# Router logits as rows times four columns, a moved statistics step, biases split on VectorE, and new unit places in a selective scan

## Chip, cores and metric

One Trainium2 chip, one of its cores. The metric is the device time of one execution in microseconds; the median of three runs of the kernel before is 1462.75 us (1462.28 to 1463.16).

## What is computed

Two layers on x of shape (2, 2048, 256), float32. Layer 0: a layer norm `xn`; a gated linear recurrence (`h = f*h + z`, five 256x256 projections of an RMS-normed `xn`) whose output is added to `xn`; times the SiLU of a top-1 mixture of 4 experts. Layer 1: a layer norm; a selective scan (512 channels, 16 states); times the SiLU of a product with binarised weights. Cut to what matters here:

```python
# layer 0, router (x here is the layer norm of the input)
logits = x @ Wr + br                       # Wr is 256 x 4
probs = softmax(logits); top_w, top_idx = top_k(probs, 1)
out = expert[top_idx](x) * top_w           # silu(x@Wg) * (x@Wu) @ Wd
# layer 1, scan over time for each of 512 channels and 16 states n
dA = exp(d_t[..., None] * A)
state = dA * state + (d_t * u_t)[..., None] * b_t[:, None, :]
y_t = einsum('bdn,bn->bd', state, c_t)
y = ys + D * xc;  y = y * silu(z);  out = y @ W_out + b_out
```

## The kernel before, in words

Every engine has an instruction list of its own, in a fixed order; engines meet through semaphores. The work goes in chunks of 512 tokens (CHUNKS = 8), each of 4 tiles of 128 tokens.

Front end (0 to 49 us). VectorE makes the sums of each tile (`tile_sums`, L944), the `statistics` of two chunks at a time (L954 to L961), waits for GpSimd's power -0.5 (L586) and scales the rows (`scaled_tiles`, L967) into two staging tiles. TensorE turns them (`turn_inputs`, L1377), ScalarE copies them to `xT` (L692), TensorE makes the logits with the 4 columns of `w_r` as the loaded operand and 512 tokens moving (`logits`, L1386). ScalarE copies the 4x512 result (`copy_logits`, L697), and TensorE turns it back to token rows in `bank7` (`turn_logits`, L1394). TensorE's order: inputs of c, logits of c-1, turned logits of c-2. VectorE reads all logits at once (L1010), finds the maximum and the one-hot (L1019); TensorE then makes the ranks (L1412, L1413) between the third and the fourth projection of mixer chunk 0 (`project`, L1434). GpSimd also makes the power for all rows (L587), then splits the output weights and the biases into bfloat16 parts (`split_output` L564 to L568, `split_biases` L575 to L580). ScalarE scales the projection weights `w0` (L707) after chunk 4.

Mixer (49 to 205 us) and experts (205 to 588 us): 8 mixer chunks, then 35 slots of 128 rows through gate and up products (L1488) and down products (L1501).

Scan (600 to 1460 us). It goes in 8 turns q (one a chunk) of 64 units u; unit u = 4n + d is state n and channel block d. In each unit TensorE turns one block of `dbuT` into bank 4 or 5 (`spread`, L1671) one unit ahead, waiting for the scan before last; VectorE runs the scan (L1328); ScalarE makes `dA` (L864) and, four units ahead, a piece of `dbuT` (L853). GpSimd multiplies four finished scans by c (L674, `hc`), preceded by a small copy (L669). TensorE sums them into y (`add_up`, L1688). For the states n in `POOL_SPREADS` GpSimd makes `dbuT` (L656) four states ahead, in ScalarE's place. Between these, the constants at L49 to L88 say in which unit each engine does a step of the next chunk (or, in `Y` and `OUT`, of the one before): X, convolution and silu (`PE_X`, `ACT_X`, `DVE_CONV`, `ACT_SILU`), gate product (`PE_G`), low-rank steps (`PE_DT`, `PE_DL`, `PE_BC`, `PE_BT`), softplus and delta (`ACT_SOFT`, `DVE_DELTA`), du on GpSimd (`POOL_DU`, L640) and its turn (`PE_DUT` L1616, `ACT_DUT` L819), z products (`PE_Z`, L1562), output (`PE_YF`, `PE_OUT`), the residual on GpSimd (`POOL_RES`, L647). These steps share banks 6 and 7: a step waits until the one before it in its bank was read. `LAST_...` constants are for turn 7.

Of the kernel before, what the change touches and what calls it, by code (L numbers as in the profile page):

```python
# [83 lines left out]
POOL_DU = (8, 10, 11, 11)  # L84
POOL_RES = (12, 13)
SUM_AT = {(13, 0): 0, (13, 1): 2, (13, 2): 2, (13, 3): 4, (14, 0): 4, (14, 1): 4, (14, 2): 6, (14, 3): 6, (15, 0): 6,
          (15, 1): 7, (15, 2): 8, (15, 3): 8, (0, 0): 13, (0, 1): 14, (0, 2): 14, (0, 3): 14, (1, 0): 14, (1, 1): 15,
# [3 lines left out]
           "YF3": 1, "BC": 1, "OUT0": 1, "OUT1": 1, "Z0": 1, "Z1": 1, "Z2": 0, "Z3": 1}  # L91

# [24 lines left out]
LAST_TURNED = (6, 7, 4, 5)  # L117
IDLE_PRODUCTS = 12
# [25 lines left out]
def build(nc, a, out):  # L144
    with ExitStack() as ctx:
# [70 lines left out]
        logitsT = rt[0:NE].rearrange("p k t e -> p (k t e)").rearrange("p (u t) -> p u t", t=CH)  # L216
# [73 lines left out]
        logits_made = sem("logits_made")  # L290
        logits_copied = sem("logits_copied")
# [22 lines left out]
        eid_ready = sem("eid_ready")  # L314
        xg_loaded = [sem(f"xg_loaded{i}") for i in range(XG_BUFS)]
# [228 lines left out]
        def _(pool):  # L544
# [25 lines left out]
            def split_biases():  # L570
                pool.wait_ge(ld_small, 16 * 4)
                biases, taken = bias_f[:, 0:3 * D].rearrange("p (b d) -> p b d", d=D), bias_f[:, 3 * D:]
                for k in range(PARTS - 1):
                    part, less = (bias_b[0:PARTS, :, half, :] for half in range(2))
                    then(pool.tensor_copy(part, biases))  # L575
                    then(pool.tensor_tensor(less, part, taken[:, k:k + 1].unsqueeze(2).broadcast_to([PARTS, PARTS, D]),
                                            ALU.mult))
                    then(pool.tensor_tensor(biases, biases, less, ALU.add))
                for half in range(2):
                    pool.tensor_copy(bias_b[0:PARTS, :, half, :], biases).then_inc(split_ready, 1)  # L580

# [8 lines left out]
            split_biases()  # L590
# [96 lines left out]
        def _(act):  # L687
# [6 lines left out]
            def copy_logits(c, u):  # L694
                act.wait_ge(logits_made, c + 1)
                wait_past(act, logits_ready, c - 1)
                act.copy(logitsT[:, u, :], bank[4 + u][0:NE, :]).then_inc(logits_copied, 1)  # L697
# [11 lines left out]
            copy_logits(CHUNKS - 1, (CHUNKS - 1) % 2)  # L709
# [1144 lines left out]
```

## Time and profile before

| what | us |
|---|---|
| median of 3 runs | 1462.75 |
| the profiled execution | 1461.61 |
| its span | 1459.8 |
| TensorE busy (share of the span) | 1408.3 (96%) |
| VectorE busy | 1026.8 (70%) |
| GpSimd busy | 915.7 (63%) |
| ScalarE busy | 895.0 (61%) |
| chain that ended last: TensorE, VectorE, ScalarE | 75%, 11%, 8% |

PE is TensorE, PEld its weight loads, DVE VectorE, ACT ScalarE, POOL GpSimd. A name such as L1386 is a line of the kernel. In the timeline a line is start, duration, engine, line, operation, what it writes and reads, how often, and in brackets how long the engine had been idle and what ended that. Where several instructions stand in one line, the duration is from the first start to the last end. A float32 product appears as two load-and-product pairs.

### The profile page before, as it was taken

The numbers are of one execution on the slowest core, as the hardware profiler recorded it, in microseconds if no ns is written. First come the engines' busy times: TensorE is split into PE (matmuls) and PEld (weight loads), VectorE is DVE, ScalarE is ACT, GpSimd is POOL, SyncE is SP. The second block draws the span as 40 slices with busy tenths as digits, with TensorE's granted clock in tenths as the row PEclk, the third lists the DMA queues.
The fourth block names the chain that finished last, engine by engine and source line by source line (L and its number), as shares of the span: only waits on it lengthen the run. The fifth ranks groups of instructions, "written<-read, shape, count | busy, mean of one in ns | idle before, by whom it ended". The sixth has DMA issues, their size and how long they took to land.

```text
span 1459.8 us, 24233 instructions
## 1 busy us (share of the span) xinstructions
PE 1408.3 (96%) x9098; PEld 1128.4 (77%) x9128; DVE 1026.8 (70%) x1373; ACT 895.0 (61%) x1465; POOL 915.7 (63%) x463
## 2 busy tenths in 40 slices
PE   6999999999999999989899999999999999999998
PEld 3454469999999999457677877878778778788887
DVE  7655542233332322588898998998998998998997
ACT  4211121111111111389989989999899899899993
POOL 4422211222222222149989989989989989899895
PEclk9999999999999999999999999999999999999999
DMA  9921136666766764110121121211211211201211
GB/s 310 395 79 47 58 115 241 254 262 232 258 259 244 271 243 155 41 59 29 45 73 45 45 74 43 73 59 43 82 37 45 88 44 45 73 31 44 88 55 47
DMA packets 53299, 172.70 MB, mean 118 GB/s; under 512 B 6079, under 2 KB 32319, under 8 KB 48326
## 3 DMA queue, kind: packets, MB, share of 16 engines
q1 hardware_dynamic: 46054, 150.22, 29.1%
q0 software_dynamic: 7136, 21.01, 4.3%
q8 instruction: 71, 1.16, 0.3%
q14 instruction: 38, 0.31, 0.1%
HBM read 141.78 MB, written 31.00 MB: 118 GB/s over the span
## 4 chain that ended last, share of the span: by engine, by line
PE 75%; DVE 11%; ACT 8%; issue 4%; POOL 1%; DMA 0%; SPq 0%; DVEq 0%; ACTq 0%; POOLq 0%
PE bank L1488 17%; PE bank L1671 10%; PE bank L1688 9%; PE bank L1434 9%; PE bank L1501 8%; DVE hst L1328 5%; PE bank L1562 4%; PE bank L1592 3%; ACT dA L864 2%; PE bank L1628 2%; PE bank L1600 2%; PE bank L1463 2%; PE bank L1555 2%; PE bank L1573 1%; ACT dbuT L853 1%
## 5 line engine op out<-in xcount | busy, mean ns | idle before, releaser
L1328 DVE TENSOR_TENSOR_SCAN hst<-dA,carry,bank 128x512 f32<-128x512 f32 x512 | 633.2, 1270 | 54.1 <-PE bank L1671 48.7
L674 POOL TENSOR_TENSOR hst<-hst,c_bc 128x2048 f32<-128x2048 f32 x127 | 579.0, 4563 | 23.0 <-DVE hst L1328 8.3
L864 ACT ACTIVATE dA<-delta,negA 128x512 f32<-128x512 f32 x512 | 360.0, 718 | 2.2 <-DVE hst L1328 1.4
L1671 PEld LDWEIGHTS bank<-ident,dbuT 128*128 128x128 f32 x2048 | 243.3, 141 | 135.8 <-issue 74.1
L1671 PE MATMUL bank<-ident,dbuT 128*128 128x128 f32 x2048 | 312.8, 276 | 15.7 <-DVE hst L1328 10.5
L1688 PE MATMUL bank<-ident,hst 128*128 128x128 f32 x2016 | 291.0, 273 | 0.0
L853 ACT ACTIVATE dbuT<-duT,bT 128x512 f32<-128x512 f32 x386 | 276.4, 717 | 1.5 <-PE bank L1671 1.4
L1488 PEld LDWEIGHTS bank<-f_sb,w_gu 128*128 128x128 f32 x2240 | 255.5, 192 | 2.7 <-ACT f_sb L736 1.0
L1488 PE MATMUL bank<-f_sb,w_gu 128*128 128x128 f32 x2240 | 256.0, 275 | 0.7 <-ACT f_sb L736 0.7
L1688 PEld LDWEIGHTS bank<-ident,hst 128*128 128x128 f32 x2016 | 234.1, 141 | 0.0
L615 POOL TENSOR_TENSOR x_sb<-x_sb,neg_half 128x1 f32<-128x1 f32 x35 | 23.0, 657 | 260.2 <-DVE x_sb L1151 260.2
L740 ACT ACTIVATE sg_z<-bank 128x512 f32<-128x512 f32 x70 | 41.9, 598 | 215.9 <-PE bank L1488 215.9
L1434 PE MATMUL bank<-xT,w 128*128 (+1 forms) x320 | 139.2, 593 | 0.0
L1434 PEld LDWEIGHTS bank<-xT,w 128*128 128x128 f32 x320 | 60.0, 190 | 71.9 <-issue 71.7
L656 POOL TENSOR_TENSOR dbuT<-duT,bT 128x2048 f32<-128x2048 f32 x31 | 112.2, 3619 | 2.2 <-PE bank L1671 2.2
L596 POOL DMA_INDIRECT sorted_x<-xn_st,idx x32 | 35.8, 1119 | 110.5 <-DVE idx L1074 103.2
L1143 DVE TENSOR_TENSOR x_sb<-x_sb 128x256 f32<-128x256 f32 x35 | 14.9, 425 | 98.7 <-ACT x_sb L751 98.7
L1132 DVE TENSOR_TENSOR xT<-sg_z,bank 128x512 f32<-128x512 f32 x36 | 24.8, 688 | 83.3 <-ACT sg_z L740 60.3
L751 ACT ACTIVATE x_sb<-bank,x_sb 128x256 f32<-128x256 f32 x35 | 16.6, 475 | 99.7 <-PE bank L1501 99.7
L1132 DVE TENSOR_TENSOR sg_a<-sg_z,bank 128x512 f32<-128x512 f32 x34 | 23.4, 688 | 76.0 <-ACT sg_z L740 50.1
L1555 PE MATMUL bank<-xn2T,w_in 128*128 128x512 f32 x128 | 66.6, 612 | 1.2 <-DVE xn2T L1224 1.2
L1501 PE MATMUL bank<-w_d,xT 128*128 x288 | 65.2, 380 | 0.8 <-ACT x_sb L751 0.8
(210 smaller groups left out, 1715.7 us busy)
## 6 DMA issues: line engine op xcount, KB each, us to landing
w_gu<-in_w_gu SPq DMA_DIRECT2D x35, 2048.0 KB
c_bc<-c_rows SPq DMA_DIRECT2D x64, 512.0 KB, 3.7
sorted_x<-sg_a SPq DMA_DIRECT2D x12, 387.0 KB, 11.3
x_sb<-sorted_x SPq DMA_DIRECT2D x35, 129.0 KB
x_sb<-in_x SPq DMA_DIRECT2D x8, 512.0 KB, 7.3
w_d<-in_w_d SPq DMA_DIRECT2D x1, 4096.0 KB, 21.1
x_mix<-x_sb SPq DMA_DIRECT2D x1, 4096.0 KB, 32.1
x_mix<-rt SPq DMA_DIRECT2D x8, 512.0 KB
```

The lines of the kernel that those rows point to most:

```text
L656: pool.tensor_tensor(dbuT[at % DBU_BUFS][:], duT[q % B][:], bT[q % B][:, :, n:n + 1].broadcast_to([P, TPC, DI]), ALU.mult).then_inc(dbuT_p ...
L674: pool.tensor_tensor(h[:], h[:], c, ALU.mult).then_inc(hc_ready, 1)
L853: act.activation(dbuT[(DS * q + n) % DBU_BUFS][:, i, :], duT[q % B][:, i, :], ACT.Copy, scale=bT[q % B][:, i, n:n + 1]).then_inc(dbuT_act, 1)
L864: act.activation(dA[:, at % DA_BUFS, :], delta[q % B][:, d, :], ACT.Exp, scale=negA[:, d, n:n + 1]).then_inc(dA_ready, 1)
L1328: v.tensor_tensor_scan(h[:, d, :], dA[:, at % DA_BUFS, :], bank[4 + u % 2][:], carry1[q % B][:, n, d:d + 1], ALU.mult, ALU.add).then_inc(s ...
L1434: ins = pe.matmul(bank[2 + w][:], w0[:, w, k, s * P:(s + 1) * P], xT[:, bass.ds((c * KB + k) * CH, CH)], start=(k == 0), stop=(k == KB - 1))
L1488: ins = pe.matmul(bank[1 + 2 * half + n][:, i * P:(i + 1) * P], w_gu[j % 2][:, n, k, at:at + P], xgT[:, k, :], start=(k == 0), stop=(k == ...
L1501: ins = pe.matmul(bank[7][:, 0:D], hidT[j % 2][:, i, :], w_d[:, bass.ds(e * (FB * D) + i * D, D)], start=(i == 0), stop=(i == FB - 1))
L1555: ins = pe.matmul(M[:], w_in[:, k, d * P:(d + 1) * P], xn2T[(t + 1) % B][:, k, :], start=(k == 0), stop=(k == KB - 1))
L1562: ins = pe.matmul(M[:], xn2T[(t + 1) % B][:, k, i * P:(i + 1) * P], w_in[:, k, DI:2 * DI], start=(k == 0), stop=(k == KB - 1))
L1671: ins = pe.transpose(bank[4 + u % 2][:, i * P:(i + 1) * P], dbuT[(DS * q + n) % DBU_BUFS][:, i, d * P:(d + 1) * P], ident[:])
L1688: ins = pe.matmul(bank[i][:, d * P:(d + 1) * P], hst[n % STATE_BUFS][:, d, i * P:(i + 1) * P], ident[:], is_transpose=True, start=False, s ...
```

## The change

The router logits are made with the turned rows as the loaded operand (128x128) and the four columns of `w_r` moving, straight into their place in `bank7`; the copy and the turning back go. TensorE's order of inputs and logits is new, ten products on the raw rows are put first, and `w0` is scaled after chunk 5. VectorE makes the last statistics between the scaling of chunks 4 and 5. The biases are split on VectorE, with one operation in place of two. In the scan stage the units of many steps change, and GpSimd makes the states 4, 7, 10, 11 in every turn. The line with `CHUNKS // 2` is the condition under which ScalarE scales `w0`. Cut to its core:

```diff
-POOL_SPREADS = (6, 7, 10, 11)
-LAST_SPREADS = (6, 7, 11)
+POOL_SPREADS = (4, 7, 10, 11)
+LAST_SPREADS = (4, 7, 10, 11)
-PE_X = (0, 1, 2, 4, 7, 8, 9, 10)
+PE_X = (0, 1, 2, 3, 7, 8, 9, 10)
-PE_DT = (22, 23, 25, 27)
-PE_DL = (28, 34, 37, 41)
-PE_BC = (27, 28, 30, 31)
-PE_BT = 44
-PE_DUT = (51, 52, 54, 56)
-PE_Z = (50, 51, 54, 55, 57, 58, 60, 61)
+PE_DT = (21, 23, 24, 26)
+PE_DL = (28, 33, 37, 41)
+PE_BC = (29, 30, 31, 32)
+PE_BT = 47
+PE_DUT = (49, 50, 53, 54)
+PE_Z = (50, 52, 53, 56, 57, 58, 60, 61)
-PE_YF = (20, 32, 36, 37)
-PE_OUT = (38, 40, 43, 44, 46, 47, 48, 49)
+PE_YF = (20, 32, 35, 37)
+PE_OUT = (39, 40, 43, 44, 46, 47, 48, 49)
-ACT_X = (5, 6, 11, 13)
-ACT_SILU = 25
-ACT_SOFT = (33, 38, 42, 45)
-ACT_DUT = (55, 56, 58, 59)
-ACT_YF = (26, 35, 39, 41)
-DVE_CONV = (3, 4, 5, 6, 7, 8, 10, 11, 12, 13, 14, 15)
+ACT_X = (5, 6, 12, 18)
+ACT_SILU = 24
+ACT_SOFT = (33, 38, 43, 44)
+ACT_DUT = (52, 53, 56, 57)
+ACT_YF = (30, 35, 40, 41)
+DVE_CONV = (3, 4, 5, 6, 7, 8, 9, 11, 12, 13, 14, 15)
-DVE_DT = 28
-DVE_DELTA = (31, 36, 40, 44)
-DVE_BC = 35
-DVE_BT = 47
+DVE_DT = 27
+DVE_DELTA = (31, 36, 41, 44)
+DVE_BC = 33
+DVE_BT = 48
-POOL_DU = (8, 10, 11, 11)
-POOL_RES = (12, 13)
+POOL_DU = (7, 9, 10, 11)
+POOL_RES = (9, 11)
...
+WARM = 10
...
-                if c == CHUNKS // 2:
+                if c == CHUNKS // 2 + 1:
...
-            two_scaled(2)
+            one_scaled(2, 0)
             statistics(3)
+            one_scaled(2, 1)
             two_scaled(3)
+            for k in range(PARTS - 1):
+                part = bias_b[0:PARTS, :, 0, :]
+                then(v.tensor_copy(part, biases))
+                then(v.scalar_tensor_tensor(biases, part, taken[:, k:k + 1], biases, ALU.mult, ALU.add))
+            for half in range(2):
+                v.tensor_copy(bias_b[0:PARTS, :, half, :], biases).then_inc(bias_ready, 1)
...
+            pe.wait_ge(ld_x[0], 16)
+            for i in range(WARM):
+                pe.wait_ge(tile_stats, min(i + 1, 2 * TPC))
+                pe.matmul(bank[7][:, 0:D], x_sb[:, 0, 0:P], x_sb[:, 0, :], start=True, stop=True)
...
-                    ins = pe.matmul(bank[4 + u][0:NE, :], w_r[:, k, :], xT[:, at:at + CH], start=(k == 0),
-                                    stop=(k == KB - 1))
+                    for k in range(KB):
+                        rows = (c * KB + k) * CH + i * P
+                        ins = pe.matmul(bank[7][:, at:at + NE], xT[:, rows:rows + P], w_r[:, k, :], start=(k == 0),
+                                        stop=(k == KB - 1))
...
+            for c in (0, 2):
+                turn_inputs(c, 0)
+                turn_inputs(c + 1, 1)
+                logits(c)
+                logits(c + 1)
+            turn_inputs(4, 0)
+            logits(4)
+            turn_inputs(5, 1)
+            for c in (5, 6):
+                turn_inputs(c + 1, (c + 1) % 2)
+                logits(c)
+            logits(7)
```

Turn 7 keeps the old `PE_YF`, `PE_OUT`, `ACT_YF` and results. The units of the sums of n = 13 to 15 and 0 move by at most one (`SUM_AT`). TensorE waits for `bias_ready` beside `split_ready` before the first mixed output.

## Rows read from the trace of the kernel before

**Rows 1.** Windows: stretch, its us, each engine's busy us, PEclk, DMA, GB/s
```profile
205.00:588.00 383.00, 381.51 (x2892) 366.17 (x2891) 118.71 (x283) 67.62 (x140) 93.18 (x102) 1.00 0.64 236
634.00:747.00 113.00, 103.74 (x667) 78.32 (x667) 102.58 (x99) 103.53 (x168) 99.02 (x42) 0.97 0.14 48
...
953.00:1056.00 103.00, 101.35 (x691) 82.42 (x692) 95.81 (x96) 96.05 (x155) 96.65 (x43) 1.00 0.18 57
```

**Rows 2.** Timeline 19 to 35 us: start, us, engine, line, out<-in, [idle before <-releaser]
```profile
19.39 1.09 PE L1377 MATMUL bank<-ident,xn_st 128*128 128x128 f32 x8
20.41 1.88 PE L1386 MATMUL bank<-xT,w_r 128*4 128x512 f32 x4
22.22 0.32 PEld L1394 LDWEIGHTS bank<-ident,rt 4*128 4x128 f32 x4 [0.86 <-issue]
29.38 2.61 ACT L707 ACTIVATE w<-w,cols 128x1280 f32<-128x1280 f32 x2
30.25 5.43 POOL L587 TENSOR_TENSOR rstd<-tmp,neg_half 128x32 f32<-128x32 f32 x1
30.32 1.39 DVE L967 TENSOR_SCALAR xn_st<-x_sb,mean,rr 128x256 f32<-128x256 f32 x4 [1.75 <-POOL rr L586]
32.91 0.19 DVE L993 TENSOR_TENSOR tmp<-tmp,rr 128x32 f32<-128x32 f32 x1
```

**Rows 3.** Timeline 40 to 63 us, all engines
```profile
40.79 1.98 PE L1434 MATMUL bank<-xT,w 128*128 128x512 f32 x4
43.25 0.29 DVE L1010 TENSOR_TENSOR rt<-bank,tmp 128x128 f32<-128x128 f32 x1 [6.97 <-PE bank L1394]
45.34 1.44 DVE L1017 TENSOR_TENSOR rt<-rt,small 128x128 f32<-128x128 f32 x1
48.54 0.49 PE L1412 MATMUL bank<-rt,z_sb 128*128 128x128 f32 x2 [1.79 <-DVE rt L1019]
49.08 13.90 PE L1434 MATMUL bank<-xT,w 128*128 128x512 f32 x32
```

**Rows 4.** Chain of work from 226.47 us: start, us, what, how many
```profile
226.47 7.14 PE bank L1488 x64
```

**Rows 5.** Waits, turn 3 (953.2 to 1056.7 us): total us, times, longest
```profile
PEld bank L1671 <- DVE hst L1328: 4.4, 13, 0.6
```

**Rows 6.** Turn 3, VectorE, ScalarE and TensorE in the timeline
```profile
951.92 0.59 ACT L781 COPY xpad<-bank 128x512 f32<-128x512 f32 x1 [2.52 <-PE bank L1555]
959.07 1.27 DVE L1328 TENSOR_TENSOR_SCAN hst<-dA,carry,bank 128x512 f32<-128x512 f32 x1
959.32 0.57 ACT L781 COPY xpad<-bank 128x512 f32<-128x512 f32 x1
971.17 1.28 DVE L1328 TENSOR_TENSOR_SCAN hst<-dA,carry,bank 128x512 f32<-128x512 f32 x1
...
1036.01 0.60 PE L1616 MATMUL bank<-ident,xpad 128*128 128x128 f32 x4
```

**Rows 7.** Turn 3, GpSimd in the timeline
```profile
964.61 0.19 POOL L669 COPY carry<-hst 128x4 f32<-128x4 f32 x1 [3.56 <-DVE hst L1328]
...
973.27 0.19 POOL L669 COPY carry<-hst 128x4 f32<-128x4 f32 x1
...
1029.99 2.53 POOL L640 TENSOR_TENSOR xpad<-delta,xc 128x512 f32<-128x512 f32 x2
```

**Rows 8.** Turn 0, TensorE in the timeline
```profile
721.40 0.66 PE L1616 MATMUL bank<-ident,xpad 128*128 128x128 f32 x4 [1.32 <-POOL xpad L640]
```

**Rows 9.** Turn 7, VectorE's and GpSimd's timelines
```profile
1374.22 4.82 DVE L1328 TENSOR_TENSOR_SCAN hst<-dA,carry,bank 128x512 f32<-128x512 f32 x4
1381.90 4.55 POOL L674 TENSOR_TENSOR hst<-hst,c_bc 128x2048 f32<-128x2048 f32 x1
...
1411.63 31.62 POOL L674 TENSOR_TENSOR hst<-hst,c_bc 128x2048 f32<-128x2048 f32 x7
```

**Rows 10.** Chain of work from 1443.49 us
```profile
1443.49 0.47 PE bank L1750 x4
```

More of the change, by code:

```diff
@@ L91 @@
            "YF3": 1, "BC": 1, "OUT0": 1, "OUT1": 1, "Z0": 1, "Z1": 1, "Z2": 0, "Z3": 1}
+LAST_SPREADS = (4, 7, 10, 11)
+LAST_PE_YF = (20, 32, 36, 37)
+LAST_PE_OUT = (38, 40, 43, 44, 46, 47, 48, 49)
+LAST_ACT_YF = (26, 35, 39, 41)
+LAST_RESULT = (45, 50)
+LAST_SUMS = {0: (14, 15, 16, 16), 1: (17, 18, 19, 19), 12: (57, 58, 59, 60), 13: (61, 62, 63, 63)}
 SUMS_AT = [[] for _ in range(UNITS)]
@@ L314, in build @@
         eid_ready = sem("eid_ready")
+        bias_ready = sem("bias_ready")
         xg_loaded = [sem(f"xg_loaded{i}") for i in range(XG_BUFS)]
@@ L568, in split_output @@
                 pool.tensor_copy(wo_b[:, 2], wo_r).then_inc(split_ready, 1)
[L570 to L580, printed above, removed]
             quarter = TILES // 4
@@ L692, in turn_inputs @@
                     act.copy(xT[:, at:at + CH], bank[2 * u + k][:]).then_inc(xrT_ready, 1)
[L694 to L697, printed above, removed]
             turn_inputs(0, 0)
@@ L838, in slot @@
                     act.preload_act_table_set("natural_log_exp_and_others")
-                if q >= 1 and u in ACT_YF:
-                    turn_y(q, ACT_YF.index(u))
+                turns = ACT_YF if q + 1 < CHUNKS else LAST_ACT_YF
+                if q >= 1 and u in turns:
+                    turn_y(q, turns.index(u))
             def spread_du(q, p):
@@ L972, in two_sums, with one_scaled @@
                 tile_sums(2 * i + 1)
+            def one_scaled(i, u):
+                v.wait_ge(rr_ready, i + 1)
+                scaled_tiles(2 * i + u, u)
             def two_scaled(i):
-                v.wait_ge(rr_ready, i + 1)
-                scaled_tiles(2 * i, 0)
-                scaled_tiles(2 * i + 1, 1)
+                one_scaled(i, 0)
+                one_scaled(i, 1)
             two_sums(0)
@@ L1271, in slot @@
                         gate_y(q - 1, DVE_GATE.index(u))
-                    if u in DVE_RESULT:
-                        result(q, DVE_RESULT.index(u))
+                    results = DVE_RESULT if q + 1 < CHUNKS else LAST_RESULT
+                    if u in results:
+                        result(q, results.index(u))
                 if q + 2 < CHUNKS and u in DVE_XN:
@@ L1379, in turn_inputs, with logits @@
                     ins.then_inc(xr_turned, 1)
-            def logits(c, u):
+            def logits(c):
                 pe.wait_ge(xrT_ready, KB * c + KB)
-                wait_past(pe, logits_copied, c - 1)
-                for k in range(KB):
-                    at = (c * KB + k) * CH
-                    ins = pe.matmul(bank[4 + u][0:NE, :], w_r[:, k, :], xT[:, at:at + CH], start=(k == 0),
-                                    stop=(k == KB - 1))
-                ins.then_inc(logits_made, 1)
-            def turn_logits(c, u):
-                pe.wait_ge(logits_copied, c + 1)
                 for i in range(TPC):
                     at = (c * TPC + i) * NE
-                    ins = pe.transpose(bank[7][:, at:at + NE], logitsT[:, u, i * P:(i + 1) * P], ident[0:NE, 0:NE])
+                    for k in range(KB):
+                        rows = (c * KB + k) * CH + i * P
+                        ins = pe.matmul(bank[7][:, at:at + NE], xT[:, rows:rows + P], w_r[:, k, :], start=(k == 0),
+                                        stop=(k == KB - 1))
                 ins.then_inc(logits_ready, 1)
-            turn_inputs(0, 0)
-            turn_inputs(1, 1)
-            logits(0, 0)
-            for c in range(2, CHUNKS):
-                turn_inputs(c, c % 2)
-                logits(c - 1, (c - 1) % 2)
-                turn_logits(c - 2, c % 2)
-            logits(CHUNKS - 1, (CHUNKS - 1) % 2)
-            turn_logits(CHUNKS - 2, CHUNKS % 2)
+            for c in (0, 2):
[10 more added lines that the diff above has]
+            logits(7)
             def ranks():
@@ L1450, in mixer @@
                 if isinstance(c, int) and c == 0:
-                    pe.wait_ge(split_ready, 3)
+                    pe.wait_ge(split_ready, 1)
+                    pe.wait_ge(bias_ready, 2)
                 pe.wait_ge(gated_ready, SB * c + SB)
@@ L1642, in slot @@
                     dt(q, PE_DL.index(u))
-                if q >= 1 and u in PE_YF:
-                    turn_y(q, PE_YF.index(u))
+                turns = PE_YF if q + 1 < CHUNKS else LAST_PE_YF
+                if q >= 1 and u in turns:
+                    turn_y(q, turns.index(u))
                 if q + 1 < CHUNKS and u in PE_BC:
                     low_rank(q, "BC", XR - P, P, PE_BC.index(u))
-                if q >= 1 and u in PE_OUT:
-                    out_proj(q, *divmod(PE_OUT.index(u), TPC))
+                outs = PE_OUT if q + 1 < CHUNKS else LAST_PE_OUT
+                if q >= 1 and u in outs:
+                    out_proj(q, *divmod(outs.index(u), TPC))
                 if q + 1 < CHUNKS and u == PE_BT:
```

15 lines of the change are left out of this document (5 added, 10 removed).

## The prediction

> **What bounds the kernel now.** I read the stretches first, then the front end's timeline, then one whole turn of the scan. In the expert stage TensorE is busy 381.51 of 383 us, and the mixer before it runs its products without a gap [rows 1, 3]: whatever arrives earlier at 49 us reaches the scan stage whole. In the front end (to 49 us) two things end last in turn. TensorE works off a backlog: each chunk costs it 1.02 us of turned inputs (19.39 to 20.41), 1.81 of logits (to 22.22) and 0.34 of turning them back (to 22.56), 3.17 in all [rows 2], and it gets to its first projection at 40.79; VectorE has waited 6.97 us for the logits by 43.25, and TensorE then waits 1.79 for the one-hot before its rank product at 48.54 [rows 3]. In the scan stage a turn takes 103.5 us, of which TensorE is busy 101.35 in a window of 103 [rows 1]. Its load unit waits only 4.4 us a turn for VectorE's scans [rows 5], mostly in the first units, where VectorE's convolutions make it the slower engine. New places can win part of these waits and no more.
>
> **Front end.** VectorE. The last statistics are made after the first of two chunks' scaling. The 1.75 us wait for GpSimd's power [rows 2] then has 1.3 us (four scaled tiles; 1.39 with its tail) of scaling over it, so the last scaling ends at about 31.65, not 33.0.
>
> TensorE. Turning back (0.34) goes. The logits become 4 tiles x 2 halves; the trace shows two load-and-product pairs for each float32 product, so 16 pairs a chunk. The cost of a pair with four columns isn't in the trace. From above: 128x128 loads under 128 columns of products come every 7.14/64 = 0.11 us [rows 4]. From below: four loads of 128 columns before 4-column products take 0.32, 0.08 each [rows 2]. I take 0.10, between two near ends: 1.6 us a chunk (1.3 to 1.8). With 1.0 for the turned inputs that is 2.6 against 3.17, and TensorE no longer has a backlog: it follows VectorE.
>
> The Trainium skill (TensorE: Matmul & The Clock Gate, LDWEIGHTS) has a load cost columns/1.2 ns whatever the rows: 107 ns here, 1.7 us a chunk; the 0.08 of a load of four rows [rows 2] speaks against it. By the page the first projection would start 0.2 us later than below.
>
> Tail. Chunk 5 is turned by about 30.5 and copied by 31.1 (its logits' neighbour, chunk 4, goes first). ScalarE now scales the projection weights there, 2.61 us [rows 2], to 33.7. Then it makes four copies of 0.53 (to 35.75). Logits 6 run 34.75 to 36.35, logits 7 to 37.95 (37.0 with 0.08). The first projection starts there instead of at 40.79. Three projections follow: 32 records in 13.9, so 1.74 each [rows 3], to 43.15; ranks 0.54 (48.54 to 49.08), to 43.7. Before: 49.08. That is 5.4 us, if VectorE's one-hot is there by 43.15.
>
> VectorE to the one-hot. The bias split comes to it: two casts and two three-operand operations on 768 elements, then two casts. No row shows them on VectorE. From above, 256 elements take 0.34 (1.39 for four) [rows 2], so 768 take 1.0: six, 6.3 with their waits. From below 0.19 each, the row of 32 elements: 1.2. I take 4.5, because the 256-element row is the nearer and casts can be quicker. From 31.65 it ends at 36.2 (32.9 to 38.0); the scale product of the logits takes 0.7 more, with the second power ready at about 34.5. The logits arrive at 38.0, so it is hidden but for the upper end. From the logits to the one-hot it took 5.3 (43.25 to 48.54), with one operation of 1.44 where its like takes 0.29 [rows 3]: GpSimd's bias operations ran beside it, and they go. I take 3.1, so 41.2: 2 us of slack (none at 5.3 and the upper end; then 0.9 of the 5.4 is lost). Next late is TensorE itself. GpSimd's split of the output weights still ends (38.9) before ScalarE's first sigmoid. The ten new products on the raw rows end by about 13.4 even at half speed and touch nothing that ends last: 0, at worst 0.5 hidden under the sums. No DMA moves, save that the expert loads are issued 5 us earlier. Front: -5.4, from -6.3 to -4.5.
>
> What VectorE meets from GpSimd: a two-operand operation took 0.19 at 32.91, inside GpSimd's power of 5.43 (30.25 to 35.68) [rows 2]. So the power doesn't block it. The Trainium skill (SBUF — State Buffer, SBUF: two separate sides) says that VectorE operations with two SBUF inputs and GpSimd operations lock each other out for a whole instruction; by it the split would wait for the power's end (about 34.4) and end near 39, and the front would win some 4.5 to 5.4. That row speaks against it for the power, the 1.44 for it elsewhere.
>
> **Scan places, turns 1 to 6.** (a) ScalarE's third copy goes from unit 11 to 12, 0.61 later, and VectorE's convolution of it from unit 10 to 9. In the old timing the tap would be ready at 959.32+0.61+1.34 = 961.3 and VectorE there at 959.07+1.19 = 960.26: 1.0 short, in the part where VectorE is the slower. But ScalarE had idled 2.52 for TensorE's second product [rows 6], which moves up a unit, 1.4 us. So the tap is at 959.9: hidden, 0.35 in hand. (b) GpSimd makes the spread of n=4 in the 3.56 us gap before n=2, instead of n=6 after it; n=3 then waits for the scan of unit 15 (971.17+1.19) and starts at 972.5 instead of 973.27 [rows 6, 7]: 0.77. From there to the last two du products it took 56.72. (c) Ahead of the last du now stand one du and one residual more, 1.25 each (2.53 for two): 972.5+56.72+3x1.25 = 1033.0. TensorE turns it two units earlier: 1036.01 [rows 6] less two spreads with sums (1.74), less a half z product (0.87), less 0.3 that smoother units win = 1033.1. The slack falls from 3.5 to 0.1 us. What TensorE gains ahead of that point is capped there: -0.3 a turn, -1.8 in six. Bounds: all 1.7 us of TensorE's waits gone, or 0.5 later. (d) The other shifts by a unit or two keep TensorE's sum of work over a turn; that their producers come in time too is what the bounds are for.
>
> Turn 0: TensorE waited until 721.40 for the third du in unit 54 [rows 8]. The fourth now comes at about 721.3 in the same unit, but half a z product and a turn (1.3) that followed are already done: -1.3 (0 to -1.6).
>
> Turn 7: GpSimd works without a gap to 1443.25, and TensorE takes its last product at 1443.49 [rows 9, 10]. It gets four spreads for three: +3.6. The one made early fills a gap, so n=3 starts with the scan's end at 1379.05 instead of 1381.90: -2.85. Net 0.75 less the 0.2 of slack: +0.55 (0 to +1.1).
>
> **The sum:** -5.4 -1.3 -1.8 +0.55 = -8.0 us. The profiled execution took 1461.61 with a span of 1459.8; the span becomes 1451.8, the execution 1453.6. The median of the runs is 1.14 above the profiled one: 1454.8.
>
> **Rivals.**
> - A late fourth du: GpSimd's row of three is 0.5 us longer and every turn waits for it, so a turn changes by +0.2 instead of -0.3, turn 0 too: -5.4+0.55+7x0.2 = -3.5, 1459.3. For: slack 0.1. Against: all its terms are rows. 0.17, on both sides of the bound.
> - The late tap of (a): ScalarE doesn't come earlier. 7x1.08 = +7.6; -5.4+0.55+7.6 = +2.8: 1465.5. Against: its idle of 2.52. 0.08.
> - The turned logits don't do what they say: the load isn't hidden and costs its whole recorded time, up to 0.19: 3.0 us a chunk, TensorE keeps a backlog of 4.0 a chunk from 22.6 to 46.1, +2.7 at 49 us; with the scans 1463. Against: the 0.11 of rows 4. 0.07.
> - The scan gains all it can: 1.7x7 = -12: 1445. Against: the du chain. 0.06.
 Against: between them lie 2.6 us of work a chunk. 0.06.
>
> **How the numbers follow.** Forecast 0.56. About 0.2% (2.9 us) is what a measurement can tell. Faster: the forecast, the full gain and half of the du case, 0.71. Same: the other half, the unhidden loads, part of the tap case, 0.20. Slower: the clock and the rest, 0.09. Range 1449.0 to 1463.5: the forecast with its bounds (front 0.9 each way, turns -1.7 to +0.5), the du and the load cases; outside stay the full gain, the tap and the clock.
>
> **What would show it.** The rank product at 43 to 44 us without a wait for VectorE; logits of 1.3 to 1.8 us a chunk; VectorE's bias operations under 6.3 together and before the logits; the expert stage 5.4 earlier with its length unchanged; turns of 103.2 us, TensorE's turn of the fourth du with a wait of a few tenths for GpSimd; GpSimd's last product ending 0.8 later against turn 7's start. I am wrong if the one-hot is late, the turns grow, or PEclk falls before 49 us.

## The result

| | before | after |
|---|---|---|
| median of 9 runs each, us | 1462.71 (1461.04 to 1463.16) | 1465.83 (1464.21 to 1470.40) |
| ratio, 95% interval | | 1.0029 (1.0021 to 1.0038) |
| profiled execution / its span, us | 1461.61 / 1459.8 | 1464.96 / 1462.9 |
| mean granted TensorE clock | 0.997 | 0.987 |

By the medians the change makes the kernel 3.1 us slower (the interval of the ratio is 3.1 to 5.6 us); the forecast was 1454.8 (1449.0 to 1463.5), 11 us lower than what was measured.

**Where the time went.** I follow five marks through the traces: the projections that start behind the rank product, the first expert's product, the same convolution step of VectorE in each turn (its distance is the length of a turn), and the start of VectorE's last operation. In us:

| kernel | projections | to first expert | to turn 0 | turn 0 | turns 1 to 5, each | turns 6 and 7 | end |
|---|---|---|---|---|---|---|---|
| before | 49.08 | 158.04 | 436.64 | 101.48 | 103.55 | 194.29 | 1457.26 |
| after | 53.01 | 158.04 | 436.59 | 101.65 | 103.20 | 195.04 | 1460.33 |

So the front end lost 3.93, turn 0 0.17 and the last two turns 0.75; turns 1 to 5 won 0.35 each. The front end alone turns the forecast round: -5.4 was expected.

The same stretches of the front end in the windows of the kernel after (columns as in [rows 1]; before had a granted clock of 1.00 in all of them):

```profile
16.00:19.00 3.00, 2.84 (x26) 2.75 (x25) 3.00 (x10) 0.04 (x1) 1.34 (x1) 1.00 0.99 373
19.00:23.00 4.00, 3.44 (x19) 3.44 (x19) 3.79 (x17) 1.75 (x3) 0.74 (x1) 0.57 1.13 294
23.00:27.00 4.00, 4.00 (x33) 4.00 (x34) 3.84 (x15) 0.59 (x2) 0.90 (x1) 0.87 1.14 287
27.00:31.00 4.00, 3.33 (x17) 2.92 (x15) 3.08 (x11) 1.17 (x2) 3.46 (x2) 0.50 1.08 275
31.00:36.00 5.00, 5.00 (x25) 5.00 (x26) 1.27 (x4) 1.94 (x3) 3.66 (x1) 0.50 1.21 228
41.00:50.00 9.00, 9.00 (x26) 6.00 (x27) 5.22 (x15) 1.60 (x3) 0.82 (x1) 0.51 0.95 399
```

PEclk (third from the end) falls to 0.5, the 1.2 GHz level, in most of 19 to 50 us (36 to 41, not shown, has 0.84), although TensorE is busy for nearly all of it. TensorE's and VectorE's timelines of the kernel after, to be held against [rows 2, 3]:

```profile
15.21 3.63 PE L1391 MATMUL bank<-w_r,xT 128*128 128x4 f32 x32
19.56 1.97 PE L1381 MATMUL bank<-ident,xn_st 128*128 128x128 f32 x8 [0.72 <-DVE xn_st L952]
22.82 3.93 PE L1391 MATMUL bank<-w_r,xT 128*128 128x4 f32 x32
38.78 6.19 PE L1391 MATMUL bank<-w_r,xT 128*128 128x4 f32 x32
44.83 7.90 PE L1435 MATMUL bank<-xT,w 128*128 128x512 f32 x12
53.01 7.46 PE L1435 MATMUL bank<-xT,w 128*128 128x512 f32 x17
...
36.02 0.93 DVE L986 CAST bias_b<-bias_f 3x768 bf16<-3x768 f32 x1
36.99 1.84 DVE L987 SCALAR_TENSOR_TENSOR bias_f<-bias_b,bias_f 3x768 f32<-3x768 bf16 x1
45.11 0.29 DVE L1009 TENSOR_TENSOR rt<-bank,tmp 128x128 f32<-128x128 f32 x1 [1.61 <-PE bank L1391]
```

At the full clock 32 pairs with four columns take 3.63, or 0.113 each; the last 32 take 6.19. The turned inputs double from 1.09 to 1.97, and the 12 records of the first projections take 7.90 where 5.2 was expected. The one-hot is quick (2.4 from 45.11; 5.3 before) and TensorE does not wait for it, as forecast, but all of it stands 7 us later than forecast (45.11 for 38.0).

### The profile page after: what moved, and what is told of

Read it like the earlier page. It is cut to its first block, busy times and chain, and to the rows that moved or that the text cites. A ratio compares the mean times of both kernels' runs of the same rounds, so it can differ in the third digit from the quotient of the medians.

```text
span 1462.9 us, 24412 instructions
## 1 busy us (share of the span) xinstructions
PE 1419.6 (97%) x9212; PEld 1152.5 (79%) x9212; DVE 1030.1 (70%) x1379; ACT 886.7 (61%) x1453; POOL 911.0 (62%) x456
## 4 chain that ended last, share of the span: by engine, by line
PE 79%; DVE 8%; ACT 5%; issue 4%; POOL 2%; DMA 0%; POOLq 0%; SPq 0%; DVEq 0%; ACTq 0%
PE bank L1489 17%; PE bank L1674 11%; PE bank L1691 11%; PE bank L1435 10%; PE bank L1502 8%; DVE hst L1328 4%; PE bank L1593 4%; PE bank L1563 3%; PE bank L1629 3%; ACT dA L849 2%; PE bank L1601 2%; PE bank L1574 2%; POOL hst L665 1%; PE bank L1465 1%; ACT dbuT L838 1%
## 5 line engine op out<-in xcount | busy, mean ns | idle before, releaser
L1674 PEld LDWEIGHTS bank<-ident,dbuT 128*128 128x128 f32 x2048 | 246.3, 142 | 141.4 <-issue 89.3
L838 ACT ACTIVATE dbuT<-duT,bT 128x512 f32<-128x512 f32 x382 | 271.7, 712 | 11.7 <-PE bank L1674 11.6
L647 POOL TENSOR_TENSOR dbuT<-duT,bT 128x2048 f32<-128x2048 f32 x32 | 115.7, 3614 | 0.8 <-PE bank L1674 0.7
L735 ACT ACTIVATE x_sb<-bank,x_sb 128x256 f32<-128x256 f32 x35 | 16.6, 473 | 99.7 <-PE bank L1502 99.7
```

The source lines that it names most:

```text
L647: pool.tensor_tensor(dbuT[at % DBU_BUFS][:], duT[q % B][:], bT[q % B][:, :, n:n + 1].broadcast_to([P, TPC, DI]), ALU.mult).then_inc(dbuT_p ...
L838: act.activation(dbuT[(DS * q + n) % DBU_BUFS][:, i, :], duT[q % B][:, i, :], ACT.Copy, scale=bT[q % B][:, i, n:n + 1]).then_inc(dbuT_act, 1)
L1674: ins = pe.transpose(bank[4 + u % 2][:, i * P:(i + 1) * P], dbuT[(DS * q + n) % DBU_BUFS][:, i, d * P:(d + 1) * P], ident[:])
```

## The experiments

All times beside runs of the kernel before on the same chip (medians 1462.06 to 1462.53).

| kernel | median (range), us | ratio, 95% interval |
|---|---|---|
| new scan places only | 1461.11 (1459.01 to 1461.51) | 0.9988 (0.9979 to 0.9998) |
| new front end only | 1468.68 (1465.36 to 1471.61) | 1.0048 (1.0033 to 1.0064) |
| after, 128 columns moved | 1457.75 (1454.97 to 1458.37) | 0.9966 (0.9954 to 0.9977) |
| after, old logits | 1460.05 (1459.84 to 1460.94) | 0.9988 (0.9979 to 0.9998) |
| after, old logits, no early products | 1459.72 (1459.13 to 1460.20) | 0.9984 (0.9975 to 0.9994) |
| after, no early products | 1471.09 (1465.36 to 1473.96) | 1.0060 (1.0040 to 1.0081) |
| 128 columns, three last spreads | 1457.34 (1455.62 to 1457.91) | 0.9962 (0.9948 to 0.9977) |
| 128 columns, late expert loads | 1455.70 (1455.39 to 1456.57) | 0.9956 (0.9942 to 0.9970) |
| 128 columns, biases on GpSimd | 1459.38 (1458.08 to 1460.85) | 0.9979 (0.9969 to 0.9988) |
| 128 columns, no early products | 1456.58 (1455.84 to 1458.27) | 0.9961 (0.9947 to 0.9975) |
| combination | 1455.40 (1454.50 to 1456.70) | 0.9955 (0.9941 to 0.9969) |
| combination, old places | 1457.07 (1456.44 to 1457.80) | 0.9965 (0.9953 to 0.9977) |
| combination, residuals at 12 and 13 | 1453.94 (1453.38 to 1454.23) | 0.9943 (0.9928 to 0.9958) |
| before, late expert loads | 1461.97 (1461.27 to 1462.54) | 1.0001 (0.9991 to 1.0010) |

**1. How many columns the products move.** The kernel after, with each logits product 128 columns wide; 124 of them multiply zeros, and what they give is overwritten by later tiles or read by nobody.

```
+ v.memset(w_rw[:], 0.0)                       # VectorE, at the start
+ v.tensor_copy(w_rw[:, :, 0:NE], w_r[:])      # behind the second two_sums
- pe.matmul(bank[7][:, at:at + NE], xT[:, rows:rows + P], w_r[:, k, :], ...)
+ pe.matmul(bank[7][:, at:at + P], xT[:, rows:rows + P], w_rw[:, k, :], ...)
```

> The kernel after, but each logits product moves 128 columns and not 4: VectorE zeroes a 128x2x128 tile and copies the router's 4 columns into it, TensorE writes 128 columns of PSUM of which the first 4 count. Same waits, same order, same number of products; the 120 idle columns fit beside the weight load (an estimate from 0.136 us for a turned 128x128 against 0.113 for a pair with 4 columns). Theory 1 (the clock fell because the products moved only four columns): the granted clock stays at 1.00 in 16 to 50 us, the first projection stands near 36 to 38.5 us, the total is 1457 to 1459 us. Rival 2 (it fell because TensorE waits for VectorE between the chunks): the clock falls as in the kernel after, the first projection stands at 44 to 46 us, 1465.5 to 1467 us. Rival 3 (the biases on VectorE are what is late, not the clock): the clock stays full but the first projection moves by no more than the 2 us of the turned inputs, 1463 to 1464 us.

Windows and timeline of this kernel:

```profile
16.00:19.00 3.00, 2.62 (x24) 2.43 (x22) 3.00 (x10) 0.00 (x0) 1.02 (x1) 1.00 0.98 370
19.00:23.00 4.00, 3.56 (x30) 3.32 (x31) 3.79 (x17) 2.15 (x4) 1.06 (x1) 1.00 1.12 268
31.00:36.00 5.00, 4.45 (x40) 4.21 (x39) 4.89 (x8) 4.69 (x7) 4.92 (x3) 1.00 1.17 205
...
14.89 3.74 PE L1400 MATMUL bank<-w_rw,xT 128*128 128x128 f32 x32
19.25 1.09 PE L1388 MATMUL bank<-ident,xn_st 128*128 128x128 f32 x8 [0.62 <-DVE xn_st L955]
38.44 5.32 PE L1444 MATMUL bank<-xT,w 128*128 128x512 f32 x12
44.04 13.90 PE L1444 MATMUL bank<-xT,w 128*128 128x512 f32 x32
```

TensorE is about as busy as in the kernel after (2.62 and 3.56 against 2.84 and 3.44) and has about the same wait before the second chunk pair's turned inputs (0.62 against 0.72), but the clock stays at 1.00. The extra columns cost 0.11 per 32 pairs. The first projection starts at 38.44, the next ones at 44.04: 5.04 us before the kernel before, 8.97 before the kernel after (0.32 of this stands at the first turned inputs already, 12.76 against 13.08: executions start a little differently). This is theory 1, and the median is 8 us under that of the kernel after. The forecast's front end, 37.95 and 43.7, was right but for its clock.

**2. Waits, the early products, and why the times lie so far apart.** The old form of the logits in the frame of the kernel after, with and without the ten early products, and the kernel after without them.

```
- turn_inputs(c, 0); ...; logits(c); logits(c + 1)              # after
+ turn_inputs(c, c % 2); logits(c - 1, ...); turn_logits(c - 2, ...)   # as before
```
```
- for i in range(WARM): ... pe.matmul(bank[7][:, 0:D], x_sb[:, 0, 0:P], x_sb[:, 0, :], ...)
```

> The kernel after with the old form of the logits (w_r as the weights, 512 columns moved, ScalarE's copy, four turns per chunk) and its old order on TensorE and ScalarE; the early products on TensorE, the statistics between two chunks' scaling, the biases on VectorE and the new scan places stay. Theory 1: the granted clock is full throughout the front end as in the kernel before, so the first projection stands where before had it or up to 2 us later (the bias split of VectorE is then what ends last), 38 to 43 us from the span's start; 1460 to 1464 us. Rival 2 (the moved statistics or the early products make the clock fall): it falls here too and the time is 1465 us or more.

> The kernel after with the old form of the logits and without its ten early products. Theory (in the run with them the fall at 19 to 23 us was that of a TensorE that had waited 2.38 us for VectorE, because its turned inputs had ended sooner): the first turned inputs take 1.9 us per 8, TensorE is not idle in 16 to 19 us, the clock is 1.00 in 19 to 23 us, and the next projections start within 0.5 us of 48.29; 1460 us. Rival (the fall there has nothing to do with the wait): it is there in this run too.

> The kernel after without its ten early products. Theory 1 (the four-column products alone let the clock fall): the granted clock still falls to half in 26 to 50 us, the next projections start at 52 to 53.5 us, 1465 to 1466 us. Rival (the fall needs the early products' head start and TensorE's waits that follow from it): the clock stays full, the next projections start near 44, 1457.5 us.

> The four-column form without the early products, one more profiled execution. Theory (a longer execution is one in which the clock stays at half for longer, or falls again behind the front end): a time of 1469 us or more comes with longer stretches at half clock than in the first profile. Rival (the further 5 us are lost elsewhere, with the clock full): they are in the mixer, where the first chunk's scatter ends later, or in the scan's turns. If the execution is a short one (1465 to 1466 us) nothing is learnt.

> The new front end with the old scan places, one more profiled execution. The same two theories: at 1469 us or more, either longer stretches at half clock in the front end, or a loss behind it with the clock full; at 1465 to 1467 us nothing is learnt.

With the old form and the early products, TensorE idles 2.38 us and the clock then is at half once, which theory 1 had not expected:

```profile
16.00:19.00 3.00, 0.88 (x3) 0.00 (x0) 3.00 (x10) 0.57 (x1) 1.05 (x1) 1.00 1.00 371
...
19.00:23.00 4.00, 3.73 (x11) 1.88 (x12) 3.79 (x17) 1.17 (x2) 1.04 (x1) 0.57 1.12 275
...
19.27 1.97 PE L1391 MATMUL bank<-ident,xn_st 128*128 128x128 f32 x8 [2.38 <-DVE xn_st L962]
```

Without the early products that wait is 0.87 and the clock 1.00 from its first entry at 16.6 us to the end of the front end; the next projections start at 46.84 instead of 48.29. That was over 0.5 earlier, because at the full clock TensorE works its backlog off sooner. So with the old form the fall goes with the wait, and the wait comes with the early products. In the kernel after neither is the cause. Without the early products its clock falls in the same stretches (0.57 in 19 to 23, 0.50 in 27 to 36), the next projections start at 53.16, and TensorE has no gap ahead of the first fall:

```profile
16.00:19.00 3.00, 3.00 (x30) 3.00 (x28) 3.00 (x10) 0.72 (x2) 0.97 (x1) 1.00 1.00 370
19.00:23.00 4.00, 4.00 (x24) 4.00 (x24) 3.79 (x17) 1.61 (x3) 1.11 (x1) 0.57 1.11 262
```

The times of a four-column kernel lie 6 to 9 us apart from execution to execution, those of the others 1 to 3.5. Without early products two of five executions took 1465.4 and 1465.6 and three 1471.1 to 1474.0, so the median misses my 1465 to 1466. A second profiled execution without early products took 1472.02 us (the one of the kernel with the new front end took 1466.96, a short one, and showed nothing new). Its windows and timeline:

```profile
19.00:23.00 4.00, 4.00 (x20) 4.00 (x21) 3.79 (x18) 0.00 (x0) 0.26 (x1) 1.00 1.10 321
23.00:27.00 4.00, 4.00 (x20) 4.00 (x21) 3.52 (x11) 1.65 (x3) 1.38 (x1) 1.00 1.10 293
...
17.00 6.83 PE L1387 MATMUL bank<-w_r,xT 128*128 128x4 f32 x32
23.68 1.95 PE L1377 MATMUL bank<-ident,xn_st 128*128 128x128 f32 x8
52.64 7.28 PE L1431 MATMUL bank<-xT,w 128*128 128x512 f32 x12
60.20 13.90 PE L1431 MATMUL bank<-xT,w 128*128 128x512 f32 x32
```

The first 32 pairs take 6.83 instead of 3.84: TensorE keeps from its start to about 42 us the pace of the 1.2 GHz level. PEclk prints 1.00 there only because the trace's list of granted clocks has no entry yet: its first one, with the full level, is at 42.8 us, and at 15.9 in the first execution; the pace changes at these times. So in the long execution the clock rose 27 us later. The next projections start at 60.20 instead of 53.16. Of these 7.0 us, 0.85 stand at the first turned inputs already (13.56 against 12.71), and the rest is the clock; from there to the end both take 1407.2 to 1407.4. The theory (longer at half) holds. Of the kernel after and of the one with the new front end only short executions were profiled. Their long ones have the lower mean clocks (0.984 at 1470.4 against 0.988 at 1464.2; 0.985 at 1471.6 against 0.988 at 1466.1), which fits more time at half, but where it lies is not shown.

**3. The two halves apart.**

```
places only:    before + the new constants and the LAST_ ones
front end only: after  - the new constants
```

> The kernel before with the new places of the scan stage alone (the front end is the old one: old logits, statistics and biases). Theory A (the front end lost 3.9 us and the scan places gave back some 0.8 net, each by itself): the first scan starts where it did before (633.7), turns 0 to 6 end about 1.5 to 2.5 us early, the last turn gives about 0.9 back; 1461 to 1462 us, some 1.3 us under before. My forecast's own sum for these parts: turn 0 -1.3, turns 1 to 6 -1.8, turn 7 +0.55, so 1460.2. Rival (the extra half-clock stretch in turn 0 of the kernel after is a consequence of the new places): turn 0 gains nothing here either and 1461.5 or more comes out; if it is a consequence of the late front end, turn 0 gains its 1.3 here.

> The kernel after with the old places of the scan stage: only the front end is new. Theory A: the first projection stands at 44.8 us from the span's start against 40.8 before, the granted clock is at half in about 19.5 to 23 and 26 to 50 us, and everything behind runs 3.9 us late: 1466.6 us. Rival (the scan places and the front end are not independent): under 1465 or over 1468.5.

| kernel | projections | to first expert | turn 0 | turns 1 to 5, each | turns 6 and 7 |
|---|---|---|---|---|---|
| places only | 49.11 | 158.04 | 101.78 | 103.25 | 195.00 |
| front end only | 52.91 | 158.04 | 102.08 | 103.54 | 194.27 |

Turns of 103.2 belong to the places, the late projections to the front end. The front end alone came out at 1468.68, above its expected 1466.6 and the bound of the rival; its profiled execution is a short one with 1466.10, and three of its six took 1470.8 to 1471.6 (experiment 2). Turn 0 gains nothing with the new places alone, with the clock at 0.57 in 715 to 719 where it had been 1.00: the half-clock stretch in turn 0 comes with the new places, as the rival had it. Turn 0 is also where the halves don't add up: +0.30 and +0.60 against +0.17; the part on the prediction says why.

**4. Who takes back what the front end won.** In experiment 1 the way from the projections to the first expert takes 159.81, not 158.04. VectorE's timeline names the wait:

```profile
74.15 1.38 DVE L1076 TENSOR_SCALAR xn_st<-x_sb,mean,rstd 128x256 f32<-128x256 f32 x4 [5.03 <-DMA sorted_x<-xn_st,idx]
```

The second chunk's rows need the buffer that the first chunk's scatter (GpSimd's DMA that puts the rows in the order of the experts) reads. The kernel before has the same wait, shorter:

```profile
76.24 1.38 DVE L1070 TENSOR_SCALAR xn_st<-x_sb,mean,rstd 128x256 f32<-128x256 f32 x4 [2.08 <-DMA sorted_x<-xn_st,idx]
```

The scatter shares the 16 DMA engines with two loads of 2 MB; the DMA share is 1.10, 1.04 and 0.97 in the five-us stretches from 60 to 75. Two kernels with these loads behind the second mixed chunk:

```
- load_up(0); load_up(1)
- with sp.Fori(0, CHUNKS - 1) as c: store_mixed(c)
+ store_mixed(0); store_mixed(1); load_up(0); load_up(1)
+ with sp.Fori(2, CHUNKS - 1) as c: store_mixed(c)
```

> The 128-column form of the logits, and the two loads of expert weights (2 MB each, issued at 53.5 us) issued behind the second mixed chunk's store (about 82 us), so that the first chunk's four scatters have the DMA engines nearly for themselves. Theory A (the mixer took back 1.8 of the 5.0 us won in front because VectorE waited until 74.15 us for the first chunk's scatter, and that landing is set by what the 16 DMA engines move until then): VectorE's wait of 5.0 us before the second chunk's rows falls to under 2 us, the first expert's product stands 1.5 to 2 us earlier (202.0 against 203.85), 1456.0 us. Rival (the scatter takes its time whatever else moves): the wait stays at 4 to 5 us and the time at 1457.7 us. Second rival (the expert weights are then late at the first expert): no, they have 110 us of cover; if it were so the first expert would start later than 203.85.

> The kernel before, with the two loads of expert weights alone issued behind the second mixed chunk's store. Theory A (in the kernel before the first chunk's scatter is waited for too, 2.08 us, but the projections of TensorE cover all of it but 0.25): the wait is gone and the first expert's product stands at 206.9 to 207.1 against 207.12, the time is the same, 1462.2 to 1462.5 us. Rival (the scatter costs the kernel before as much as it costs the one with the fast front end): 1460.7 us.

VectorE and the windows with the 128-column form and late loads:

```profile
69.38 1.38 DVE L1078 TENSOR_SCALAR xn_st<-x_sb,mean,rstd 128x256 f32<-128x256 f32 x4
...
65.00:70.00 5.00, 5.00 (x13) 2.28 (x12) 4.29 (x8) 0.64 (x2) 0.33 (x1) 1.00 0.44 164
```

The wait is gone, the share falls to 0.44, and the way to the first expert is 158.04 again (44.38 to 202.42): 1.77 us, and 2.05 in the medians. In the kernel before the same edit takes away its wait of 2.08 as well and gives nothing (158.03; ratio 1.0001): there TensorE's projections cover it. Theory A holds in both.

**5. Biases on GpSimd or on VectorE.**

```
- VectorE:  tensor_copy, scalar_tensor_tensor (twice), two tensor_copy
+ GpSimd:   split_biases() behind split_output(), as before
```

> The 128-column form of the logits, with the biases split on GpSimd as in the kernel before. Theory A (with the clock full, VectorE's split of 6.7 us ends within 1 us of the last logits, so it costs at most that; and the mixer's wait for the scatter eats what is won in front): the next projections start at 43.2 to 43.6 us against 44.04, the first expert's product stands where it was (203.85), total within 0.4 us of 1457.7. Rival (the split on VectorE is worth what the change put it there for): the front end is not earlier or the ranks wait for GpSimd, 1458.5 us or more.

I expected almost nothing and it costs 1.6 us in the medians. In the marks it is 2.8 (projections 45.09, first expert at 206.69 for 203.85), of which 0.6 stand at the first turned inputs already (13.36 for 12.76), so 2.2. VectorE and GpSimd in its timeline:

```profile
40.58 1.19 DVE L1022 TENSOR_TENSOR rt<-rt,rs 128x128 f32<-128x128 f32 x1
42.01 1.61 DVE L1025 TENSOR_TENSOR rt<-rt,small 128x128 f32<-128x128 f32 x1
45.85 3.47 DVE L1036 TENSOR_TENSOR_SCAN rt<-rs,rt 128x32 f32<-128x32 f32 x4
...
40.16 1.46 POOL L582 TENSOR_TENSOR bias_b<-bias_b,bias_f 3x768 bf16<-3x768 bf16 x1
41.70 1.76 POOL L584 TENSOR_TENSOR bias_f<-bias_f,bias_b 3x768 f32<-3x768 f32 x1
44.42 1.46 POOL L582 TENSOR_TENSOR bias_b<-bias_b,bias_f 3x768 bf16<-3x768 bf16 x1
```

A VectorE operation of 0.29 ends 0.15 us behind GpSimd's two-operand operation that was under way: 41.77 behind 41.62, and 43.62 behind 43.46. The four scans take 3.47 instead of 1.01. The Trainium skill (SBUF — State Buffer, SBUF: two separate sides) says that a VectorE operation with two SBUF inputs waits for the whole of such a GpSimd operation; for these operations the trace agrees ([rows 2] has one of 0.19 inside GpSimd's power, which did not wait). So this part of the change is worth 1.6 to 2.2 us once the front end is early: the rival was right against me. The forecast had this gain in its one-hot (5.3 to 3.1); it was my expectation for this run that forgot it.

**6. The last turns, the residuals, the places.** The combination is the 128-column form with late loads, three spreads on GpSimd in the last turn and no early products.

```
a. 128 columns:  LAST_SPREADS = (4, 7, 10, 11) -> (6, 7, 11)
b. 128 columns:  without the ten early products
c. combination
d. combination:  all old scan places
e. combination:  POOL_RES = (9, 11) -> (12, 13)
```

> The 128-column form of the logits, and in the last turn the three spreads on GpSimd of the kernel before (6, 7, 11) and not four. Theory A (what the last turn loses is its fourth spread on GpSimd): everything up to the last turn as in the run of the 128-column form (its last turn's start is where it was), turns 6 and 7 cost 0.7 less, 1457.0 us. Rival (turn 6's lateness, not the last turn's own places, is what costs): the same 1457.7 us.

> The 128-column form of the logits without the ten early products on x. Theory A (the early products do nothing for the clock, which stood at full in the kernel before without them): clock 1.00 from 11 to 50 us, first projection at 38.4, 1457.7 us. Rival (they lift the clock before the first turned inputs): the first turned inputs and products run at half clock, the front end is 1 to 3 us later unless VectorE hides it, 1458 to 1460 us.

> The 128-column logits, the loads of expert weights behind the second mixed chunk, three spreads on GpSimd in the last turn, and no early products. Theory A (each saving stands by itself: front end 5.0, mixer 1:1 again, turns 1 to 5 0.3 each, last turn 0): 1455.0 us, 7.5 under before. Rival (what is won in front changes where the clock falls in turn 0, which has been worth up to 0.8 either way): 1454.5 to 1456.

> The kernel of the run before this one, with all the old places of the scan stage. Theory A (the new places are worth 0.33 a turn in turns 1 to 5, about nothing in turn 0): a turn of 103.55 us and not 103.2, 1.7 us more than that run, 1456.7 us. Rival (my forecast's turn 0 gain of 1.3 is there with a fast front end): 3 us more.

> The same combination, with the two residuals of GpSimd at 12 and 13 as in the kernel before and not at 9 and 11. My forecast's theory (the residual at 11 stands ahead of the fourth du and makes TensorE's turn of it wait some 0.2 us a turn): turns 1 to 6 are 0.2 us shorter each, 1.0 to 1.2 us in all. Rival (the 0.2 us wait of TensorE is not on the path of the scan): the same within 0.3 us. Second rival (the places 12 and 13 then collide with the next turn's spreads): slower by up to 1 us a turn.

| kernel | projections | to first expert | turn 0 | turns 1 to 5, each | turns 6 and 7 | end |
|---|---|---|---|---|---|---|
| 128 columns | 44.04 | 159.81 | 102.22 | 103.20 | 195.04 | 1453.70 |
| a | 44.57 | 159.81 | 101.99 | 103.25 | 194.25 | 1453.52 |
| b | 44.20 | 159.23 | 101.20 | 103.23 | 195.04 | 1452.39 |
| c | 44.16 | 158.04 | 102.01 | 103.20 | 194.19 | 1451.00 |
| d | 44.48 | 158.03 | 101.44 | 103.53 | 194.34 | 1452.56 |
| e | 44.50 | 158.04 | 101.21 | 103.00 | 194.25 | 1449.60 |

(a) The fourth spread on GpSimd costs the last two turns 0.79, about the 0.75 that the forecast set against it; the medians (1457.34 and 1457.75) are too near to tell. (b) The early products do lift the clock before the first turned inputs (1.07 instead of 1.94), which I had not expected, but VectorE hides it: the projections start at 44.04 with them and at 44.20 without. (d) Old places: 0.33 a turn more in turns 1 to 5, as forecast, and no gain of 1.3 for the new ones in turn 0. (e) The units 12 and 13 take away TensorE's wait for the fourth du. TensorE's load unit, waits in turn 3, the kernel after and then c (e has no such row):

```profile
PEld bank L1617 <- POOL xpad L631: 0.2, 1, 0.2
...
PEld bank L1624 <- POOL xpad L636: 0.2, 1, 0.2
```

A turn goes from 103.20 to 103.00 in all five, the 0.2 of that row. The ends of c and e are 1.4 apart: 1.0 from these turns, 0.8 from turn 0, where the clock was at half for less time, and 0.4 lost at the start and the end. With e the kernel takes 1453.94, 8.2 us under the kernel before: faster than both.

## Why the prediction was wrong, point by point

**TensorE's clock: the step that failed.** The sum ran all of the front end at the full clock. The half-clock rival stood at 0.06 with 1475; it is what happened, at a lower price: 8.97 us (53.01 against 44.04), where the rival had 20 over the forecast. Its reason was wrong as well. I named TensorE's waits; experiment 1 keeps the waits and about the busy time and the clock stays, and without the early products it falls with no gap ahead of it (experiment 2), so it is the four moved columns. The text's own argument against the rival, "between them lie 2.6 us of work a chunk", does not hold for four-column products: the clock fell with 4.00 of 4.00 us busy (experiment 2). No row of before shows 128x128 loads with four moved columns; 0.06 was far too low for an operation form that I had only priced by its duration.

**The front end otherwise.** Pair 0.10 expected, 0.113 measured. Tail: 37.95 and 43.7 expected, 38.44 and 44.04 measured with the clock full, a gain of 5.04 for 5.4 (the 37.0 given for pairs of 0.08 adds up to 37.3). One-hot 3.1 expected, 2.4 measured. The bias split was sized at 4.5, with 6.3 as its upper end; it takes 7.1 (36.02 to 43.11), and 6.75 in experiment 1. The narrow three-operand operations take 1.01 alone and 1.84 or 2.00 beside GpSimd's split of the output weights: the contention that I had put aside by a row of GpSimd's power. It was hidden all the same, as the sum had it.

**"Whatever arrives earlier at 49 us reaches the scan stage whole": wrong by 1.77.** The mixer passes on a delay whole (3.93 in the kernel after), but not this gain: behind busy DMA engines the scatter comes only 2.09 earlier (74.15 against 76.24) where VectorE comes 5 earlier. The wait of 2.08 stood in the trace of before, and I had not priced what lies under its cover. With the clock full, the change comes to 1457.75, not 1454.8.

**Turn 0: the wait went, the time didn't.** TensorE's wait of 1.32 for GpSimd [rows 8] is gone. In its place the second du's turn waits for ScalarE's copy, longer than before. TensorE in the kernel before and then after:

```profile
717.70 0.63 PE L1616 MATMUL bank<-ident,xpad 128*128 128x128 f32 x4 [0.79 <-ACT duT L819]
...
718.30 0.63 PE L1617 MATMUL bank<-ident,xpad 128*128 128x128 f32 x4 [2.10 <-ACT duT L803]
718.77 1.79 PE L1563 MATMUL bank<-w_in,xn2T 128*128 128x512 f32 x2
```

0.79 for the second du and 1.32 for the third make 2.11 before, 2.10 in one piece after. Measured from the start of the turn, TensorE comes to the second du 4.6 earlier (716.20 less 647.64 against 716.91 less 643.76), but ScalarE's copy of the first, whose bank it needs, only 3.3 earlier. And right behind this wait the granted clock is at half from 718.9 to 722.3: the z product takes 1.79 where it takes 1.02 at 723.06. That costs about 1.7, an estimate from the starts of this product and the three operations behind it against the same ones in the next unit. All 13 executions with the new places have the one wait of 2.10 to 2.14 and the fall behind it, all 5 with the old ones two shorter waits and no fall. So the step -1.3 failed twice: I asked when the fourth du would be made and not when the bank of the second would be free, and I ran the turn at the full clock. Over all kernels turn 0 took 101.4 to 102.1 with old places and 101.0 to 102.2 with new ones; most of this range goes with another half-clock stretch, near the start of the turn. Where it is short (646.7 to 650.1 in the kernel before), turn 0 takes 101.44 to 101.48 with old places and 101.20 to 101.24 with new ones, so they win 0.24 like for like. Where it is twice as long (647.2 to 654.0 in the kernel after), turn 0 takes 102.06 to 102.08 with old places and 101.03 (with part of the stretch ahead of the turn) to 102.22 with new ones. Why it is long in one execution and short in another is open.

**Turns 1 to 5: right.** -0.3 forecast, -0.35 measured, with the du cap and its wait of 0.2 as forecast; experiment 6e shows the cap by lifting it.

**Turns 6 and 7.** -0.3 and +0.55 make +0.25; +0.75 was measured. The last turn is nearly right. In the kernel after:

```profile
1371.17 1.27 DVE L1328 TENSOR_TENSOR_SCAN hst<-dA,carry,bank 128x512 f32<-128x512 f32 x1
...
1381.38 4.56 POOL L665 TENSOR_TENSOR hst<-hst,c_bc 128x2048 f32<-128x2048 f32 x1 [0.55 <-DVE hst L1328]
...
1437.30 9.04 POOL L665 TENSOR_TENSOR hst<-hst,c_bc 128x2048 f32<-128x2048 f32 x2
```

The same scan of VectorE stood at 1368.91 in the kernel before, so all is 2.26 late here. GpSimd's n=3 at 1381.38 is 1379.12 in the old timing, forecast 1379.05; its end at 1446.34 is 0.83 later than the old one in the same measure, forecast 0.75 less 0.2 of slack. The slack wasn't there. The rest is turn 6: the marks are 2.32 late at its start and 2.26 at its end, so it won 0.06 and not 0.3. Why it wins less than the turns before it I have not traced.

**The other rivals.** Late tap, late fourth du, unhidden loads and the full gain didn't happen: turns of 103.20 exclude the first two and the last, 0.113 a pair the third.

## What to carry to other kernels

A form that makes the moved side tiny can be cheap by its own durations and still cost its neighbours half their pace: if the operation count allows, try the same product with more moved columns; here 128 in place of 4 cost 0.11 us per 32 pairs and kept the clock (nothing between was run). Before crediting a stage with passing on a gain, list the waits in it that are covered today and ask which are set by something that doesn't move; a delay passes through where a gain does not. When a wait is taken away, look at the neighbour that shares its buffer: in turn 0 two waits became one of the same 2.1 us, and the clock fell behind it.

## What the runs showed of the hardware that was not expected

- TensorE that is busy without a gap, but with products of four moved columns, falls to the 1.2 GHz level: granted 0.50 in 31 to 36 us with 5.00 of 5.00 us busy. With 128 columns in the same places: 1.00 with 4.45 busy.
- It falls behind waits too: of 2.38 us in the front end with the old logits, and of 2.10 to 2.14 in turn 0 with the new places (13 of 13 executions), where two waits of 0.79 and 1.32 had left it at 1.00.
- PEclk can print 1.00 while the pace is that of 1.2 GHz: 32 pairs in 6.83 us, 8 turned inputs in 1.95. The trace has no entry of the clock before its first change (42.8 us there; 18.7 in the kernel before, whose first 8 turned inputs take 1.94). Up to that entry the durations tell.
- How long it stays at half differs between executions of the same kernel: the first rise at 15.9 and at 42.8 us, the same mark at 53.16 and at 60.20.
- VectorE's 128x128 operations of 0.29 us take up to 1.61 beside a GpSimd operation with two operands.
